# First attention with 64-wide diagonal squares in five units a batch

## What is computed

```python
# first attention: 16 heads of 8, rotary q and k, causal, no softmax
s1 = jnp.einsum('bqhd,bkhd->bhqk', q1, k1)
s2 = jnp.einsum('bqhd,bkhd->bhqk', q2, k2)
pattern = jnp.where(causal[None, None], s1 / D * (s2 / D), 0.0)
y = jnp.einsum('bhqk,bkhd->bqhd', pattern, v).reshape(B, T, C)
return y @ Wout.T
# first experts: top 2 of 8 by sigmoid, gelu, biases up_b and down_b
x = x + s * g          # g = silu(experts and shared expert)
```

## Times and profile of the kernel before

| | us |
|---|---|
| median of 3 runs (lowest, highest) | 1614.5 (1612.2, 1617.2) |
| the profiled execution | 1612.6 |
| its span | 1611.4 |
| TensorE busy in the span | 1517.2 (94%) |
| VectorE, ScalarE, GpSimd busy | 981.5, 986.3, 831.8 |
| scores' matmuls of the first attention (L1684), busy | 233.8 |

### The profile page before, as it was taken

The page is one execution under the profiler, slowest core; times in us unless marked ns, Lnnn a source line. Parts: engine busy times, 40 slices in busy tenths (PEclk is TensorE's granted clock), DMA queues, the critical chain, the costliest instruction groups (busy, mean ns, idle before and its releaser), DMA issues.

```text
span 1611.4 us, 46794 instructions
## 1 busy us (share of the span) xinstructions
PE 1517.2 (94%) x18059; PEld 1107.6 (69%) x18059; DVE 981.5 (61%) x2063; ACT 986.3 (61%) x2039; POOL 831.8 (52%) x908
## 2 busy tenths in 40 slices
PE   7999999999999999999999889999998999999895
PEld 5545454555544999999778656666666999997663
DVE  6788898877776222222599968756664222225887
ACT  5766666777766555445455557677776545455773
POOL 7334488888875555555112210277764555553433
PEclk9999999999999999999999989999999999999998
DMA  9910002110002899999344320011113545532434
GB/s 314 418 66 2 7 30 78 51 32 30 30 26 36 217 247 253 253 247 240 92 118 118 85 56 3 15 48 47 47 43 55 95 91 99 93 76 80 133 108 126
DMA packets 296954, 169.45 MB, mean 105 GB/s; under 512 B 198080, under 2 KB 273216, under 8 KB 293792
## 3 DMA queue, kind: packets, MB, share of 16 engines
q1 hardware_dynamic: 246608, 128.32, 29.8%
q0 software_dynamic: 16832, 34.64, 6.3%
q10 hardware_dynamic: 33296, 3.50, 1.9%
HBM read 96.74 MB, written 69.63 MB: 103 GB/s over the span
## 4 chain that ended last, share of the span: by engine, by line
PE 63%; POOL 12%; issue 10%; DVE 7%; ACT 4%; DMA 2%; SPq 1%; POOLq 0%; DVEq 0%; ACTq 0%
PE ps L1880 14%; PE ps L1871 14%; POOL xd L630 6%; POOL s_S L663 4%; PE ps L1684 4%; PE ps L1775 4%; PE ps L1812 4%; PE ps L1912 4%; ACT s_PX L889 3%; PE ps L1900 3%; DVE s_RS L1350 3%; PE ps L1708 2%; PE ps L1822 2%; PE ps L1841 2%; PE ps L1648 2%
## 5 line engine op out<-in xcount | busy, mean ns | idle before, releaser
L630 POOL DMA_INDIRECT xd<-s_XN,s_slots x256 | 251.7, 983 | 83.9 <-issue 62.3
L823 ACT ACTIVATE s_S<-ps 128x512 f32<-128x512 f32 x384 | 208.4, 595 | 141.3 <-PE ps L1684 141.3
L1538 DVE TENSOR_TENSOR s_PP<-ps,s_S 128x1024 f32<-128x1024 f32 x192 | 234.4, 1221 | 74.1 <-PE ps L1684 52.7
L1684 PE MATMUL ps<-s_QM,s_KK 32*128 32x512 f32 x1536 | 233.8, 639 | 2.7 <-ACT s_S L823 2.7
L889 ACT ACTIVATE s_PX<-ps,s_scl 128x1024 f32<-128x1024 f32 x128 | 135.7, 1111 | 110.5 <-PE ps L1822 110.5
L904 ACT ACTIVATE s_HH<-ps,s_LG 128x256 f32<-128x256 f32 x284 | 125.2, 474 | 122.0 <-PE ps L1871 122.0
L663 POOL TENSOR_SCALAR_AFFINE_SELECT s_S<-s_S 128x1024 f32<-128x1024 f32 x128 | 140.8, 1100 | 114.0 <-ACT s_S L823 113.4
L647 POOL DMA_INDIRECT yd<-s_Y,s_to x142 | 136.2, 959 | 122.2 <-DVE s_Y L1480 97.8
L1350 DVE TENSOR_REDUCE s_RS<-ps 128x8 f32<-128x1024 f32 x128 | 150.3, 1216 | 63.3 <-PE ps L1779 63.3
L904 ACT ACTIVATE s_XN<-ps,s_b1s 128x256 f32<-128x256 f32 x256 | 113.4, 474 | 115.1 <-PE ps L1871 111.1
L647 POOL DMA_INDIRECT yd<-s_XN,s_to x128 | 122.7, 959 | 117.5 <-DVE s_XN L1480 95.6
(11 more groups left out here) (222 smaller groups left out, 2737.1 us busy)
## 6 DMA issues: line engine op xcount, KB each, us to landing
s_W<-in_ew SPq DMA_DIRECT2D x71, 576.0 KB, 4.6
s_X<-xd SPq DMA_DIRECT2D x540, 32.0 KB
xd<-s_zero SPq DMA_DIRECT2D x16, 1056.0 KB, 18.1
s_YG<-yd SPq DMA_DIRECT2D x32, 256.0 KB, 3.6
s_XN<-yd SPq DMA_DIRECT2D x32, 256.0 KB, 4.0
yd<-s_zero SPq DMA_DIRECT2D x7, 1056.0 KB, 27.9
s_XN<-in_x SPq DMA_DIRECT2D x8, 512.0 KB, 7.2
xd<-s_XN,s_slots POOLq DMA_INDIRECT x256
```

Of the source, the lines that this page charges most:

```text
L630: e.indirect_dma_start(out=xd, out_offset=bass.IndirectOffsetOnAxis(ap=m.slots[:, k, i:i + 1], axis=0), in_=m.XNp[:, i, 0:C + 1], in_offse ...
L823: e.mul(m.S1[u % 3][:, t * 512:(t + 1) * 512], m.PA[:, t * 512:(t + 1) * 512], 1.0 / 64.0).then_inc(s.ev1, 1)
L1538: e.tensor_tensor(m.PP[u % 4][:], m.PB[u % 2], m.S1[u % 3][:], ALU.mult).then_inc(s.prod, 1)
L1684: return e.matmul(out, m.KK[k][32 * r:32 * r + 32, kind, kc * P:(kc + 1) * P], m.QM[k][32 * r:32 * r + 32, kind, :, qc * P:(qc + 1) * P], ...
```

## The change

The causal squares on the diagonal are cut once more, at 64. Of each 128 by 128 square, the upper right quarter of (keys, queries) is all masked and needs no work. What is left is the low quarter (queries 0 to 63 with keys 0 to 63) and the high half (queries 64 to 127 with keys 0 to 127). The low quarters have 64 keys, and two heads' groups of them are put on the partitions 0 to 63 and 64 to 127. So a batch has five units: v = 0 holds the low quarters of both squares and all 16 heads (packed); v = 1 and 2 hold the high halves of both squares, 8 heads each; v = 3 and 4 hold the pair across, as before.

The weighing follows in three parts: packed (32 matmuls of 64 rows, 32 columns of weights, 64 moving columns, in two steps of 16), high (32 matmuls of 64 moving columns) and across (16 of 128). For the packed part the values of every second group of heads are needed on partitions 64 to 127; `moved_values`, new on SyncE, copies them there by four DMAs a batch, from the kept values `RS` to a third plane of `VM`. The GpSimd selection runs on units 0, 1, 2 (the packed unit twice, the second time over 64 partitions). The up biases of the experts now lie behind the other weights of an expert in DRAM (1156 words a row, 1152 before) and are read from there, and the VectorE steps that spread them go. The tables of the routing steps are set anew for five units a batch.

```diff
-NU = NB * 6
+UB = 5
+NU = NB * UB
-ROUTED_BY = [6, 7, 8, 9]
+ROUTED_BY = [5, 6, 7, 8]
-EW = 2 * HID + C
+EW = 2 * HID + C + 4
...
+def moved_values(e, m, s, b):
+
+    g = b // 2
+    e.wait_ge((s.va, s.vd)[g % 2], g // 2 + 1)
+    e.wait_ge(s.zvm, 3)
+    if b >= 1:
+        e.wait_ge(s.pv, 3 * (b - 1) + 1)
+    for h in range(4):
+        src = m.RS[0:64, b * 256:b * 256 + 256].rearrange("p (k r h d) -> p r h k d", k=4, r=2, h=4)[:, 1, h, :, :]
+        e.dma_start(m.VM[b % 2][64:128, 2, h:16:4, 8 * h:8 * h + 8], src).then_inc(s.v2, 16)
...
     e.wait_ge(s.const, 96)
-    e.dma_start(m.upb[:], a["up_b"].rearrange("e (p j) -> p e j", j=4)).then_inc(s.upb, 16)
     e.dma_start(m.r0.low[:], a["c_low"].bitcast(BF16)).then_inc(s.const, 16)
     e.dma_start(m.r0.ones[:], a["c_ones"].bitcast(BF16)).then_inc(s.const, 16)
-    e.wait_ge(s.zero, 272)
-    e.wait_ge(s.zero_y, 128)
-    turn_counts(e, m, s, m.r0, 0)
-    for i in range(m.x0.NWB):
-        expert_weights(e, m, s, i)
+    for b in range(NB):
+        moved_values(e, m, s, b)
+        if b == 0:
+            e.wait_ge(s.zero, 272)
+            e.wait_ge(s.zero_y, 128)
+        if b == ROUTED_BY[0] - 1:
+            turn_counts(e, m, s, m.r0, 0)
+        if b == 10:
+            for i in range(m.x0.NWB):
+                expert_weights(e, m, s, i)
...
-    sel = m.S1[u % 3][:].rearrange("p (b q) -> p b q", q=P)
+    sel = m.S1[u % 3][:].rearrange("p (b q) -> p b q", q=64)
...
+    if u % UB == 0:
+        low = sel[0:64, :, :]
+        e.wait_ge(s.mask, 4 * (u // UB) + 1)
+        e.affine_select(out=low, in_=low, pattern=[[0, 16], [1, 64]], compare_op=ALU.is_ge, fill=0.0, base=0,
+                        channel_multiplier=-1).then_inc(s.mask, 1)
...
+def scores_packed(e, m, k, kind, out, t):
+
+    for x in range(2):
+        for half in range(2):
+            r, at = 2 * t + half, P * x
+            i = e.matmul(out[64 * half:64 * half + 64, 256 * x:256 * x + 256], m.KK[k][32 * r:32 * r + 32, kind, at:at + 64],
+                         m.QM[k][32 * r:32 * r + 32, kind, :, at:at + 64], start=True, stop=True, skip_group_check=True)
+    return i
+
+
+def scores_high(e, m, k, kind, out, r):
+
+    for x in range(2):
+        i = e.matmul(out[:, 256 * x:256 * x + 256], m.KK[k][32 * r:32 * r + 32, kind, x * P:(x + 1) * P],
+                     m.QM[k][32 * r:32 * r + 32, kind, :, x * P + 64:(x + 1) * P], start=True, stop=True, skip_group_check=True)
+    return i
...
     def scores(n, kind, t):
-        k, pair, r = (n // 6) % 2, (n % 6) // 2, 2 * (n % 2) + t
-        kc, qc = (0, 0, 1)[pair], (0, 1, 1)[pair]
+        k, v = (n // UB) % 2, n % UB
         out = (m.PB[n % 2] if kind else m.PA)[:, t * 512:(t + 1) * 512]
-        return e.matmul(out, m.KK[k][32 * r:32 * r + 32, kind, kc * P:(kc + 1) * P],
-                        m.QM[k][32 * r:32 * r + 32, kind, :, qc * P:(qc + 1) * P], start=True, stop=True)
+        if v == 0:
+            return scores_packed(e, m, k, kind, out, t)
+        if v < 3:
+            return scores_high(e, m, k, kind, out, 2 * (v - 1) + t)
+        return scores_across(e, m, k, kind, out, 2 * (v - 3) + t)
...
+def weigh_packed(e, m, s, b, heads):
+
+    PP = m.PP[(UB * b) % 4]
+    e.wait_ge(s.prod, UB * b + 1)
+    e.wait_ge(s.vm, b + 1)
+    e.wait_ge(s.v2, 64 * (b + 1))
+    if b >= 1:
+        e.wait_ge(s.yt, b)
...
-    for u in range(-1, NU + 4):
-        v, b = u % 6, u // 6
+    for u in range(-1, NU + 2):
+        v, b = u % UB, u // UB
...
+        if v == 1 and b >= 1:
+            weigh_across(e, m, s, b - 1)
...
+        if v == 2 and b + 1 < NB:
+            projection(e, m, s, b + 1, 3)
+        if v in (2, 3) and b < NB:
+            weigh_packed(e, m, s, b, (2 * v - 4, 2 * v - 3))
+        if v == 3 and b + 2 < NB:
+            projection(e, m, s, b + 2, 0)
+        if v == 4:
+            weigh_high(e, m, s, b)
         if v == 4 and b + 2 < NB:
-            projection(e, m, s, b + 2, 0)
+            projection(e, m, s, b + 2, 1)
```

156 lines of the change are left out of this document (73 added, 83 removed).

## The result

The changed kernel took **1909.7 us** (median of 4, 1904.0 to 1917.6) where the kernel before took 1613.4 (1610.3 to 1617.2) beside it: a ratio of 1.184, interval 1.179 to 1.189. The forecast was 1800, its range ended at 1830: the sign was right, the size 110 us too small, and the range did not hold it.

A forecast was written before the change was run, and what follows sets the result against it. TensorE's instructions in order were taken to bound the first attention. From 1612.6 us, 156 for longer batches, 28 for a first pause and 3 for the clock gave about 1800 us; range 1645 to 1830, holding 0.79.

The forecast's parts named there:

- The bound: First attention: TensorE's instructions in their order set the pace, 14.24 us a batch; savings on VectorE and ScalarE booked at nothing.
- A mixed step, 4.24: Score steps v = 0 and v = 4: each shape drains before the next, 2 x (1.07 + 1.05) = 4.24 us.
- The batch, 19.3: One first-attention batch: three plain steps, two mixed steps, weighing, projections and a 0.2 us wait make 19.3 us.
- The first pause, 28: First batch: TensorE waits from 63 to 91 us for moved values queued on SyncE behind 25 writes of zeros, 28 us.
- The clock, 3 us (0 to 5): Behind the first batch's pause TensorE's clock falls to 0.50 for a while, adding 3 us.
- The sum: Whole kernel: 1612.6 + 156 for the longer batches + 28 for the pause + 3 for the clock, about 1800 us.
- 1 (3.19 a step): Mixed steps: shapes on disjoint rows overlap in queue order, three phases, 3.19 us a step, 1732 us; chance 0.15.
- 2 (1.93): Mixed steps: full concurrency, 1.93 us a step, batch 14.7 us, total 1654 us; chance 0.22.
- Rival 3: Steps v = 1, 2: a row group issued twice running blocks the others, 61 us more, 1861 us; chance 0.06.
- Rival 4: Packed phases: two row groups can't write one bank at once, 110 us more in all, 1910 us; chance 0.04.
- Rival 5: First attention: the TensorE-ScalarE-TensorE loop of a unit, not TensorE, sets the pace, 2.37 us a unit, 1564 us; chance 0.08.
- The scatters, booked at nothing: GpSimd scatters coming earlier change nothing, since the expert stage starts only after the last unit; 0 us.

The follow-up runs named there:

- e5: Kernel before, with only the experts' up biases laid behind their weights and the VectorE spreading steps removed: 1663.4 us, ratio 0.9988.
- e3: Changed kernel with high halves and pair across computed as two 32 x 64 tiles each, so all scores have one shape, order unchanged: 1916.8 us, ratio 1.153.
- e4: Kernel before, with 8-column matmuls on 32 x 64 tiles put between the full-size score matmuls in two steps of each batch: 2136.1 us, single run.
- e1: Changed kernel with the first batch's moved values issued by ScalarE ahead of the zeros instead of by SyncE behind them: 2157.4 us, ratio 1.293.
- e2: Changed kernel with each step's matmuls grouped by shape, two shape changes per mixed step instead of four: 1882.7 us, ratio 1.130.
- e9: Changed kernel with matmuls grouped by shape, first moved values issued early by ScalarE, and all 128 scatters behind the first attention: 1819.1 us, ratio 1.128.
- e8: Changed kernel with GpSimd's 128 row scatters for the first experts all moved behind the first attention: 2071.1 us, ratio 1.284.
- e16: Changed kernel with one scatter in each step instead of 1, 1, 2, 2, 0, nothing else: 1984.7 us, ratio 1.195.
- e10: Changed kernel with matmuls grouped by shape, first moved values issued early by ScalarE, and one scatter in each step: 1677.6 us, ratio 1.039.
- e12: Changed kernel with matmuls grouped by shape, first moved values issued early by ScalarE, and scatters at 1, 1, 2, 1, 1: 1797.2 us, ratio 1.071.
- e11: Kernel before with its scatters bunched, 3 and 3 in two steps of a batch: 1642.8 us, ratio 1.018.
- e14: Changed kernel with grouped matmuls, early first moved values and one scatter a step, run on the chip kind where the kernel before is slower: 1754.8 us, ratio 1.053.

## Why the forecast was right and wrong, point by point

- **The bound.** Right. TensorE is busy for 79.84 to 80.00 of 80 us, so less work on VectorE and ScalarE has nothing to shorten, and the biases brought nothing (e5).
- **A mixed step, 4.24.** Right: 4.12 and 4.13. The parts were 1.07 + 1.05 twice; they are 1.05 to 1.06 and 1.01. The reason was the right one: e3 keeps rows, banks and order, changes the shape alone, and gets 2.37; e4 shows the drain where the rows are disjoint, which the rows of before did not. With the rule cited from the Trainium skill, "TensorEngine Tiling (Array Packing)", section Key Properties, that changing the mode drains the engine, the traces agree: in e4 the small matmul starts only when the one ahead of it, on other rows, has had its 1.05 to 1.17 us.
- **The batch, 19.3.** Right at full clock: 19.12.
- **The first pause, 28.** The mechanism and the queue were right; the size was 22.3. The landing was forecast for 91 and came at 89.8; the wait began at 67.5 instead of 63, since the steps ahead of it were at half clock: it had fallen at 56.2, before any pause of the stage.
- **The clock, 3 us (0 to 5). This is the step that failed.** I had read the earlier trace rows, a clock at 0.50 behind a pause, and took a pause for the only cause; so the term was laid behind the one pause that I expected. In the trace the clock is at 0.50 for whole steps while TensorE works without a gap. Batches have a mean of 23.0 where 19.1 is their full-clock length, 3.9 us a batch, 113 us over the 29 batches from the third on, where the term had 3; the first two have 72.1 us, where 2 x 19.3 + 28 = 66.6 was forecast. What the runs showed in its place: the clock falls with thin phases, without any wait, and before the pause. e1 takes the pause away, and the batches stay at 23.4 to 26.9; e2 until the scatters, and e9 against e8, thicken the phases, and it is at 1.00. The rows that I had in hand could have warned: they said what TensorE did before the clock fell in one place, not what it needs to stay up.
- **The sum.** The stage and its start were forecast 187 us longer and were 289, and the rest of the program gave 5 more. That is 107 of the 110 us; the last 3 are between the profiled run and the median. The sum also set 32 bare batches (618) against a stage that holds some 6 us of routing (462), and so was 6 short; against 113 that is nothing.
- **The rivals.** 1 (3.19 a step) and 2 (1.93) fell with the 4.12. Rival 3, a row group issued twice in a row, fell with the step v = 1 at 1.09 us. Rival 4 gave 1910, the number measured, by a mechanism that isn't there: a packed phase with two row groups in one bank lasts 1.01, not 1.91. Rival 5 fell with the bound. That the time matches a rival says nothing; its step does.
- **The scatters, booked at nothing** ("has no one waiting"). True on A by e8. On B it is false for the five-unit order: the forecast asked who waits for a scatter, and not what a scatter holds up. On B the changed kernel's ratio was 1.306, and 1.195 with the bunching undone (e16).
- **The range.** It had no case for a clock that falls under load. A term of one sign whose mechanism is known from a single row should have had its other bound: the whole stage at half clock.

What is shown of the clock, and what is not: where nothing holds TensorE up, the same matmuls in phases of four row groups keep 1.00 (e2 until the scatters, e9 and e10 from 148.4 and 145.9 us on), and in phases of one or two row groups they have 0.74 to 0.86 (the changed kernel); matmuls of full size, one at a time, have 0.72 to 0.79 (e4). Thickening the phases, by the order alone, undoes the fall. But thin phases are not the only thing that goes with it: in e2 and e12 on B the phases are full, and it falls where long rows of scatters break up the weighing. Nor do they always bring it: in e16 whole batches of thin phases, with rows of three scatters beside them, run at 1.00 and take 20.7 us. So that the order of the matmuls sets the clock here is shown, and what in it does is not. Why a thin batch now and then runs at 1.00 (433.84 to 452.96, or 320 to 400 in e16) stays open. So does what stops TensorE's issue while scatters go out, and how kinds A and B differ. The grouping with the scatters at 1, 1, 2, 2, 0 was measured on B only, so what it would give on A stays open too.

Is there a version of this change that wins? At full clock the grouped one has seven score phases of some 1.07 us a batch, since a mixed step is two, where the kernel before has six: 15.08 against 14.24. The saved unit is less than what two mixed steps add.

## What to carry to other kernels

Price a step of small matmuls by the changes of shape in its issue order and not by its columns: group what has one shape, since four thin phases cost as much as four full ones. Then ask how many row groups stream in each phase; where it is one or two, read the granted clock of the stretch, or bound the stage at half clock, even if TensorE never waits. And keep the DMAs that GpSimd issues apart from each other: when their steps are renumbered, look in the trace how many go out in a row, since one a step in the program was still three in a row in time, and ask of what stands behind them on GpSimd who waits for it (e11).

## What the runs showed of the hardware that I had not expected

- TensorE's clock falls to 0.50 while its busy share is 80.00 of 80 us (e4, 0.72 over the stretch; the changed kernel, 0.76), where phases stream on one or two of four row groups.
- Two matmuls of one shape issued 0.03 us apart in e3 overlap across row groups and banks; in e4 one small matmul of another shape, on free rows, makes full ones serial that stream at once without it.
- On B, rows of GpSimd's scatters hold up TensorE's packed weighing though the trace shows no wait between them: 4.74 us for 0.58 beside a row of five (e2). With the clock that falls behind it, that is 1.5 us a scatter in rows of five, and 0.33 in rows of three without a fall (e14). On A the same row of five costs the same weighing nothing.
- TensorE's clock also falls with full phases when they are broken up so: a mean of 0.79 in e2's batches with scatters, 1.00 in those ahead of them.
- The kernel before takes 3% more on B than on A, of which 4 us lie in the first attention.
